# Folding the memory projection into a bank weight and an output weight, reordering stage 1, one program block, and a last slot taken tile by tile

## The reference

```
xn = layernorm(x)                                         # per token, 512 features
local  = softmax(q k' / sqrt(128)) v                      # qkv = xn @ local_qkv_w
sparse = softmax over the 102 largest scores of each row  # qkv = xn @ sparse_qkv_w
xp     = xn @ memory_proj_w                               # 512 -> 128
mem    = concat(xp, softmax(xp @ bank.T) @ bank) @ mem_out_w + mem_out_b   # bank: 64 x 128
pred   = gelu((xn @ pred_in_w + b) @ pred1_w + b1) @ pred2_w + b2
s      = concat(local, sparse, mem, pred) @ warboss_w + warboss_b
g      = silu(relu(xn @ w1 + b1) @ w2 + b2)               # 512 -> 2048 -> 512
out    = x + s * g
```

## Time and profile before

| what | value |
|---|---|
| median of 3 runs | 2564.87 us (2563.07 to 2565.1) |
| the profiled execution, its own time | 2564.28 us |
| span of the profiled execution | 2562.5 us |
| mean granted TensorE clock | 0.996 |
| PE busy | 2526.4 us, 99% |
| DVE busy | 2314.5 us, 90% |
| ACT busy | 1357.4 us, 53% |
| POOL busy | 1103.7 us, 43% |

### The profile page before, as it was taken

How to read it: one execution, slowest core, us unless ns; L and a number is a source line. 1 busy time by engine, 2 the same in 40 slices (tenths; PEclk the granted TensorE clock), 3 DMA queues, 4 the chain that set the end, 5 groups by cost and what they waited for, 6 DMA issues and landing times.

```text
span 2562.5 us, 36954 instructions
## 1 busy us (share of the span) xinstructions
PE 2526.4 (99%) x12884; PEld 2142.9 (84%) x12884; DVE 2314.5 (90%) x5179; ACT 1357.4 (53%) x2304; POOL 1103.7 (43%) x851
## 2 busy tenths in 40 slices
PE   7999999899999999999999999999999999999998
PEld 6888888788888888888888888888888888888887
DVE  8666666799999999999999999999999999999995
ACT  5777777654444444444444444444444444444443
POOL 3455544433444444444444444444444444444444
PEclk9999999999999999999999999999999999999999
DMA  7787888774665466546654665466546654665443
GB/s 250 302 301 282 311 308 334 298 260 157 210 220 198 165 210 218 197 164 213 215 198 165 214 215 199 165 214 215 198 165 214 214 197 165 214 215 199 166 157 110
DMA packets 164568, 551.79 MB, mean 215 GB/s; under 512 B 17888, under 2 KB 30880, under 8 KB 156064
## 3 DMA queue, kind: packets, MB, share of 16 engines
q1 hardware_dynamic: 164384, 549.43, 61.2%
HBM read 415.15 MB, written 134.22 MB: 214 GB/s over the span
## 4 chain that ended last, share of the span: by engine, by line
PE 95%; DVE 2%; DMA 1%; ACT 0%; issue 0%; SPq 0%; POOL 0%; ACTq 0%
PE acc L67 9%; PE acc L69 9%; PE acc L68 9%; PE hid L69 9%; PE hid L67 9%; PE hid L68 9%; PE ps L67 5%; PE o L69 5%; PE o L68 5%; PE o L67 5%; PE ps L68 5%; PE ps L69 5%; PE scores L1576 4%; PE scores L67 2%; PE scores L69 2%; PE scores L68 2%
## 5 line engine op out<-in xcount | busy, mean ns | idle before, releaser
L1313 POOL TENSOR_TENSOR h_lo<-h,h_hi 128x512 fp32r<-128x512 f32 x256 | 336.4, 1314 | 819.4 <-ACT h_hi L1209 819.4
L1443 DVE MAX8 ranks<-early 128x8 f32<-128x512 f32 x819 | 564.4, 689 | 13.0
L1463 DVE MATCH_REPLACE8 early<-ranks,early 128x512 f32<-128x512 f32 x756 | 511.0, 676 | 0.0
L1208 ACT ACTIVATE h<-hid,small 128x512 f32<-128x512 f32 x256 | 176.3, 689 | 503.4 <-PE hid L69 503.4
L67 PE MATMUL acc<-w,h_hi 128*128 128x512 f32 x1024 | 411.3, 402 | 0.0
L67 PE MATMUL hid<-xnT,w 128*128 128x512 f32 x1024 | 399.0, 390 | 1.9 <-DMA w<-ffn_scratch 1.3
L69 PE MATMUL acc<-w,h_lo 128*128 128x512 f32 x1024 | 399.7, 390 | 0.0
L68 PE MATMUL acc<-w,h_hi 128*128 128x512 f32 x1024 | 399.4, 390 | 0.0
L69 PE MATMUL hid<-xnT,w 128*128 128x512 f32 x1024 | 399.4, 390 | 0.0
L68 PE MATMUL hid<-xnT,w 128*128 128x512 f32 x1024 | 398.6, 389 | 0.0
L1313 POOL TENSOR_TENSOR pT_s<-pT,pT_s 128x512 fp32r<-128x512 f32 x256 | 327.0, 1299 | 41.0 <-ACT pT_s L1221 41.0
(11 more groups left out here) (213 smaller groups left out, 5564.9 us busy)
## 6 DMA issues: line engine op xcount, KB each, us to landing
w<-ffn_scratch SPq DMA_DIRECT2D x512, 512.0 KB, 4.0
xnT_scratch<-xnT SPq DMA_DIRECT2D x16, 2048.0 KB, 13.7
kv_scratch<-kv_out SPq DMA_DIRECT2D x32, 1024.0 KB, 5.4
tile_scratch<-tiles_out SPq DMA_DIRECT2D x16, 2048.0 KB, 8.3
tl<-tile_scratch SPq DMA_DIRECT2D x64, 512.0 KB, 4.0
xnT<-xnT_scratch SPq DMA_DIRECT2D x60, 512.0 KB, 7.3
ffn_scratch<-ffn SPq DMA_DIRECT2D x16, 1024.0 KB, 6.6
values<-kv_scratch SPq DMA_DIRECT2D x16, 1024.0 KB, 6.4
```

The costliest lines, as they stand in the source:

```text
L1208: nc.scalar.activation(h32[:, c % 2, :], hid[:, :], ACT.Relu, bias=bias)
L1313: return nc.gpsimd.tensor_tensor(out_, value, hi_.bitcast(F32), ALU.subtract).then_inc(ready, 1)
L1443: l_step = count(nc.vector.max(top_l[:, own], larger[:, :]))
L1463: l_step = count(nc.vector.match_replace(larger[:, :], top_l[:, own], larger[:, :], LOWEST))
```

## The change

The projection `mp` and the scores `ms` are no longer computed for each half. At the start the kernel makes two folded weights, memory_proj_w times the transposed bank (512 x 64, `MS`) and memory_proj_w times the upper half of mem_out_w (512 x 128, `MO`). The scores are then 64 more columns beside the values: the value jobs are four, `v0` to `v3`, each 12 matmuls of 320 columns. `mo` is four products with the folded weight and two matmuls of 128 rows. DVE now copies the scores out of the four banks and takes the maximum, without the addition. The job lists have a new order. Both stages run in one block, without a meeting of the engines between them. In the last slot the four tiles are finished one after another, on DVE alone.

The diff without its changes of indentation, cut to its core:

```diff
-JOBS = ["mp", "pi", "ql", "ms", "p1a", "p1b", "qs", "kl", "wt", "ks", "p2",
-        "tr0", "tr1", "tr2", "tr3", "mo", "v01", "v23"]
-FIRST_JOBS = ["mp", "pi", "ql", "ms", "p1a", "p1b", "qs", "kl", "ks", "v01", "wt", "tr0", "p2", "tr1", "mo", "tr2",
-              "tr3", "v23"]
+JOBS = ["pi", "v0", "v1", "v2", "v3", "p1a", "p1b", "ql", "wt", "qs", "p2", "kl", "tr0", "tr1", "tr2", "tr3", "mo", "ks"]
+FIRST_JOBS = ["pi", "ql", "qs", "kl", "ks", "p1a", "p1b", "v0", "v1", "v2", "v3", "p2", "tr0", "tr1", "tr2", "tr3",
+              "wt", "mo"]
...
+        with nc.Block() as block:
+            @block.sync
+            def _(sp):
+                first.sync(sp)
+                second.sync(sp)
...
+        def scalar(act):
...
+                        if name == "v3":
+                            act.wait_ge(max_ready, n + 1)
+                            for t in range(HTILES):
+                                last = nc.scalar.activation(we[:, t, 0, :], mscore[:, t, :], ACT.Exp,
+                                                            bias=nmx[:, t:t + 1], accum_out=esum[:, t:t + 1])
+                            last.then_inc(exps_ready, 1)
...
+        def vector(dve):
...
+            def gelu_parts(n):
+                dve.wait_ge(bank_read, done(n, "p1b"))
+                nc.vector.tensor_copy(gelu_hi[:, :, :], gelu[:, :, :]).then_inc(ghi_ready, 1)
+                dve.wait_ge(ghi_ready, n + 1)
+                subtract(gelu_lo[:, :, :], gelu[:, :, :], gelu_hi[:, :, :]).then_inc(lo_ready, 1)
...
+                    if first(n):
+                        next(parts[n])
+                        next(parts[n], None)
+                        gelu_parts(n)
+                        for m, size, value in ((MS, MEM, ms32), (MO, P, mo32)):
+                            c = slice(m * P, m * P + size)
+                            dve.wait_ge(fold_out, 1 + int(m == MO))
+                            subtract(wp_lo[:, :, c], value.rearrange("p (k n) -> p k n", n=size), wp_hi[:, :, c])\
+                                .then_inc(fold_split, 1)
...
-                        dve.wait_ge(job_done, done(n, "ms"))
-                        nc.vector.tensor_copy(mscore[:, :, :], part[:, :, 1, :]).then_inc(ms_step, 1)
-                        nc.vector.tensor_tensor(mscore[:, :, :], mscore[:, :, :], part[:, :, 0, :], ALU.add)
+                    dve.wait_ge(bank_read, done(n, "v3"))
+                    own = bank(n, "v0")
+                    nc.vector.tensor_copy(mscore[:, :, :], ps[:, own:own + HTILES, 2 * P:VALUES]).then_inc(ms_step, 1)
...
+        def tensor(pe):
...
+            def folded_weights():
...
+                for k in range(KT):
+                    last = product(nc, scores[:, P + k * MEM:P + (k + 1) * MEM], mpT_hi[:, k, :], mpT_lo[:, k, :],
+                                   bkT_s[:, 0, 0, :], bkT_s[:, 1, 0, :], True, True)
...
                         elif name == "mo":
+                            for k in range(KT):
+                                product(nc, dst, wp_hi[:, k, c], wp_lo[:, k, c], xnT[:, hh, k, HI, :],
+                                        xnT[:, hh, k, LOW, :], k == 0, False)
                             pe.wait_ge(lo_ready, lo(n, "wt"))
...
-                                last = nc.tensor.matmul(dst, bm_lo[0:MEM, :], act_hi[0:MEM, WT, :], start=False,
-                                                        stop=True)
+                            last = nc.tensor.matmul(dst, bm_lo[:, :], act_hi[:, WT, :], start=False, stop=True)
+                        elif name in ("v0", "v1", "v2", "v3"):
+                            pe.wait_ge(fold_split, 2)
+                            for k in range(KT):
+                                last = product(nc, dst[:, 0:VALUES], xnT[:, hh, k, HI, c], xnT[:, hh, k, LOW, c],
+                                               wp_hi[:, k, v], wp_lo[:, k, v], k == 0, k == KT - 1)
...
                 sp.wait_ge(tiles_st, 16 * HALVES)
-                sp.wait_ge(kv_st, 32 * HALVES)
...
+            def last_tile(t):
+                m = SLOTS - HTILES + t
+                sums_of_half(HALVES - 1, (t,))
+                dve.wait_ge(sum_ready, m + 1)
+                nc.vector.tensor_tensor(mixed_of(m), mixed_of(m), gate[:, t, :], ALU.mult).then_inc(last_prod, 1)
+                dve.wait_ge(last_prod, t + 1)
+                dve.wait_ge(tanh_ready, m + 1)
+                nc.vector.scalar_tensor_tensor(out=gate[:, t, :], in0=last_tanh(t), scalar=1.0, in1=mixed_of(m),
+                                               op0=ALU.add, op1=ALU.mult).then_inc(gate_ready, 1)
...
+                nc.vector.tensor_tensor(gate[:, t, :], gate[:, t, :], residual_of(m), ALU.add).then_inc(fin_last, 1)
...
+            for t in (1, 2, 3):
+                for i in range(HC):
+                    f2(C + i, c + i, h, (t,))
```

More of the change, by code:

```diff
@@ L62, in jobs @@
     return FIRST_JOBS if n == 0 else JOBS
+ORDER = [(n, name) for n in range(HALVES) for name in jobs(n) if n < LAST or name[:2] != "tr"]
+PLACE = {job: KT + i for i, job in enumerate(ORDER)}
 def product(nc, out, w_hi, w_lo, x_hi, x_lo, first, last):
@@ L131 @@
     scores: object
-    kv_st: object
+    bank_read: object
+    k_st: object
+    v_st: object
     tiles_st: object
@@ L189, in stage1 @@
     xnT_raw, scores = shared.xnT_raw, shared.scores
[L190 to L195, removed]
+    k_st, v_st, tiles_st = shared.k_st, shared.v_st, shared.tiles_st
+    PIN, WT = range(2)
+    LO = ["pin", "gelu", "wt"]
     KV_SLOT = {"ks": 0, "kl": 1}
     SM_LOADS, BIAS_LOADS = 4, 5
+    FFN_AT = {True: "p2", False: "qs"}
     CONSTS = 3
@@ L271, in stage1 @@
         job_done = sem("job_done")
-        bank_read = sem("bank_read")
+        bank_read = shared.bank_read
         lo_ready = sem("lo_ready")
@@ new lines, in gpsimd, with lo, chunk, transposed @@
+        def gpsimd(pool):
+            def lo(out_, value, hi_, ready):
+                return nc.gpsimd.tensor_tensor(out_, value, hi_.bitcast(F32), ALU.subtract).then_inc(ready, 1)
+            def chunk(C, c):
+                pool.wait_ge(h_h, C + 1)
+                high, low = h_of(C, c)
+                lo(low, h32[:, c % 2, :], high, h_l)
+            def transposed(g, t):
+                i = 2 * g + t
+                for j in range(2):
+                    pool.wait_ge(pT_h, 2 * i + j + 1)
+                    half = slice(j * HTILES, (j + 1) * HTILES)
+                    lo(pT_s[:, half, LOW, t, :], pT[:, j, :].rearrange("p (t n) -> p t n", n=P),
+                       pT_s[:, half, HI, t, :], pT_l)
+            def head_out(g, head):
+                pool.wait_ge(at_h, g + 1)
+                lo(at_lo[:, head, :], at[:, :], at_hi[:, head, :], at_l)
+            def residual(m):
+                t = m % HTILES
+                pool.wait_ge(gate_ready, m + 1)
+                pool.wait_ge(mix_ready, m + 1)
+                nc.gpsimd.tensor_tensor(gate[:, t, :], gate[:, t, :], mixed_of(m), ALU.mult)\
+                    .then_inc(prod_ready, 1)
+                pool.wait_ge(prod_ready, m + 1)
+                pool.wait_ge(xr_in[m % 2], 8 * (m - m % 2) + 16)
+                nc.gpsimd.tensor_tensor(gate[:, t, :], gate[:, t, :], residual_of(m), ALU.add)\
+                    .then_inc(fin_ready, 1)
+            def slot(m):
+                C = c = HC * (m - 1)
+                chunk(C, c)
+                transposed(m - 1, 0)
+                chunk(C + 1, c + 1)
+                if m % 2 == 0:
+                    transposed(m - 1, 1)
+                    chunk(C + 2, c + 2)
+                    head_out(m - 1, 1)
+                    if not known_first(m, 5):
+                        residual(m - 5)
+                else:
+                    if not known_first(m, 5):
+                        residual(m - 5)
+                    chunk(C + 2, c + 2)
+                    transposed(m - 1, 1)
+                chunk(C + 3, c + 3)
+                if m % 2 == 1:
+                    head_out(m - 1, 0)
+            for m in range(1, SLOTS + 1):
+                slot(m)
@@ L1718, in program @@
+        return Programs(sync, gpsimd, scalar, vector, tensor)
 def program(nc, ins, out):
```

2176 lines of the change are left out of this document (1073 added, 1103 removed).

## The result

The changed kernel takes 2573.86 us (median of 7 runs, 2571.43 to 2574.73), the kernel before 2565.1 in the same comparison: ratio 1.0031, 95% interval 1.0022 to 1.004, so slower by 0.3%. The profiled execution took 2572.95 us, with a span of 2571.2, against 2564.28 and 2562.5: 8.7 more in either. The forecast was 2579, range 2564 to 2603.

What follows compares the result with a forecast made beforehand. PE was taken to bound the kernel: its matmuls plus the gaps between them. +16.3 + 0.6 + 10 - 4.2 - 4.0 - 4.4 = +14.3 on 2564.28 gave 2579 us, range 2564 to 2603.

Steps and rivals of the forecast that it cites:

- halves 1 to 14: Stage 1: period 30.67 us, +1.16 per half, so +16.3 us, and +0.6 more because of half 1.
- the start: Half 0, up to half 1's beginning near 57 instead of 48.48: +10 us, bounds +6 and +13.
- the hand-over: Stage 1's end to the third chunk: one block removes lost time, its weights still wait; -4.0 us, bounds 0 and -9.
- no change to speak of: Rival: cheaper start, better hand-over and slightly cheaper 320-column matmuls leave +3 us, 2567; chance 0.12.
- PE's work in a half: PE's matmuls in each half: `mp` and `ms` go, values and `mo` cost more; -0.7 us per half.
- The wait at `wt`: PE ahead of `wt` in each half: softmax ready at T+5.95, wanted at T+4.09, a gap of 1.86 us.
- rival 2: ACT loads the exponential's table ahead of the maximum, shortening the chain by 1.28 us: faster, 2559.5; chance 0.10.
- Gelu's part behind it: PE at `p2`, behind `wt`: Gelu's low part comes slightly late, about +0.08 us per half.
- Half 1: Half 1 of stage 1: DVE puts a layer norm's last part before Gelu's, +0.6 us.
- Rival 1: PE's clock falls in every half behind the gap, about 1.6 us more each: +22, 2601; chance 0.22.
- Half 15: Last half of stage 1: the gap ahead of `mo` and the half speed behind it go, -4.2 us.
- the end: After the last matmul: tiles finished one after another leave 5.9 us instead of 10.3; -4.4 us, bounds -5.3 and -3.

Runs made afterwards that it cites:

- both edits: The changed kernel with a second wait ahead of the memory exponentials, and `wt` behind `qs` with `kl` ahead of `p2`: 2569.04 us (ratio 1.0013).

## Why the prediction was right, and where it was not

The direction and the range held; the forecast was 5 us too high. That it came so near is partly luck: halves 1 to 14 came out 12.4 us lower than forecast, and the start, the hand-over and stage 2 together 7.3 higher. The first error alone would have brought the forecast to no change to speak of (2566).

- **PE's work in a half** (forecast -0.7): the pitch for 320 columns, 0.147, and `mo` (208.64 to 211.93, 3.29) came as forecast. The period less the gap at `wt` (0.79, from start to start) and the 0.08 by which `ql` starts late is 29.07: -0.44. The difference of 0.26 is unsized overhead. In part it is the first matmul behind a wait or a shorter job, which starts some 0.09 late, in more places than I counted; the rest I have not traced. Over 14 halves +3.6.
- **The wait at `wt`** is the step that failed, as the prediction put it: "Table load, four exponentials, ..." in one row behind "Copy and maximum". The runs showed that the load is not behind the maximum: a gap of 0.79 instead of 1.86, some 15 us less over 14 halves. With the old wait put back, the chain is 6.05 (forecast 5.95), so all else in that step was right to 0.1. This is rival 2's mechanism, which I gave 0.10 on the ground that ACT had stood idle in the kernel before. The row was read rightly, but its cause, a second wait in the code, is one that the change removes. The rival's price was also too high: DVE's copy and maximum take 0.9 us and the load 1.28, so the load still ends last and its place saves 1.0, not 1.28. The rule of the Trainium skill, "ScalarE: Activation LUTs", section "What ACT_TABLE_LOAD costs", of some 1.38 us of drain on top of a load finds no support here: load and first exponential are 1.29 apart (225.28, 226.57).
- **Gelu's part behind it**: named with +0.08, but -0.7 + 1.86 + 0.08 is 1.24, and the 1.16 of the sum leaves it out (1.1 us over 14 halves). `p2` starts at 232.73, straight behind its predecessor, so there was nothing to add.
- **Half 1** (forecast +0.6 on top of the others): the kernel before lost time there that no row of the prediction shows.

```profile
60.09 0.30 PE L880 MATMUL ps<-bkT_s,act_hi 128*128 128x128 f32 x1 [2.79 <-DVE act_lo L606]
```

The granted clock behind this gap is 0.61 over 4 us. From its start to its transposes half 1 took 5.1 us more than a later half in the kernel before and 3.5 in the changed one, so it gave back 1.6. Rival 1 of the prediction rested on two gaps, 2.46 and 1.28, and left this third one out.

- **The start** (+10, measured +12.9): `v0` came at 40.27, not 38.0. My sum had no row for DVE's small operations beside POOL, 1.2 us each instead of 0.16, and four of them stood in the queue (VectorE's order alone gave 2.7 back). Slow clock took 1.5 in `v0` to `v3` and 0.4 in `mo`, where 1.5 were allowed for. ACT's split of the feed-forward weight, 1.05 ahead of `wt`, had no term either, and the early table load gave 0.9 back.
- **Half 15** (-4.2, -4.3) and **the end** (-4.4, -4.7; +4.0 when undone) were right in mechanism and size.
- **The hand-over** (-4.0, -1.3, and +1.7 more in stage 2 for the slow clock behind the gap): the mechanism, SP's wait for the tiles, was right, the size was not. The load was issued 11.9 us after stage 1 ended (515.2), where I had 11. I took 5 to 6 for its landing; it took 8.1, with two loads of the same size issued just ahead of it on DMA engines whose share was 0.97 to 1.03 from 520 to 535. With `w1` ahead of them it took 5.7. My own terms (11 + 5 to 6 - 12.4) would have given 3.6 to 4.6 lost and not 5.5, so the sum held a reserve that it did not name; without it the miss would be larger by 1 to 2.
- **Rival 1**, the clock falling in each half, did not happen: the gap is 0.63, and even behind 1.62 (the table load put back) the granted clock of the next 4 us is 1.00.
- **The tests that the prediction set itself**: PE does wait at `wt`, with DVE's last copy as the releaser, but 0.63 and not 1.7 to 1.9; the period is 29.94 and not 30.7; the load starts at once behind `v3`'s evacuation and not 1 us later; half 1 starts at 61.3 and not near 57.

## What to carry to other kernels

Before you copy a stall from the old trace into the new sum, look in the code for the wait that made it, and ask whether the change keeps that wait: here one redundant wait decided where a table load stood, for 1 us in each of 13 halves. An order that puts a long chain of small operations next to its consumer wants the cover counted in matmuls: 18 stood where 22 to 23 were needed (5.07 us at 0.227), and moving `wt` one job later, with `kl` ahead of `p2`, gave back more than the change had cost. Where everything falls due at once (a first half, a last half, a hand-over), count the bytes and the other engines' queues, and after each fix look at what has become late next, on the engine that feeds the one named.

## What the runs showed of the hardware

- VectorE beside GpSimd: operations on 128x4 elements took 1.17 to 1.22 us instead of 0.16; a cast of 128x1024 elements 1.81 instead of 0.69, a subtraction of them 3.25 instead of 1.23 (half 1 of the run with `wt` later).
- TensorE's clock behind gaps, as the mean granted clock of the 4 us that follow (1.00 is 2.4 GHz, 0.50 is 1.2 GHz all the time): 0.50 behind 3.16 and 3.31 us idle, 0.57 behind 3.85 and 4.28, 0.60 behind 3.59, 0.59 behind 4.82 and 7.01, but 1.00 behind 1.62 and 2.40. In the kernel before, 2.46 idle were followed by half speed. A gap of 2.75 ahead of `wt` in half 0 was followed by 1.00 in the run with the table load put back, and by 0.65 in the one with both edits. So gaps of one length came out differently, and longer ones did not cost more clock.
- One of the 512 KB loads at the hand-over landed 8.1 us after its issue on full DMA engines; the median of the 512 loads of this kind is 4.0.
- An ACT table load takes 1.28 us. With one wait ahead of the exponential it started as soon as ACT was free (225.28, before the maximum ended at 226.17); with two it started only behind the maximum (231.96, ended at 231.88).
